# Fused post-LayerNorm block with a top-k mask: a threshold search in three steps instead of five, and a new order of setup and first steps

## The reference, cut to what matters

```python
# x: 8 x 512 x 512, so 4096 tokens of 512; W_syn 2048 x 512; W_out 512 x 2048
x = layernorm(x + x @ (W + delta_W).T)
z = x @ ternary_quant(W_syn).T + b_syn                  # 2048 columns a token
topv, _ = top_k(z, 204); thresh = topv[:, -1:]
hidden = where(z >= thresh, relu(z), 0.0)
out = layernorm(x + hidden @ ternary_quant(W_out).T + b_out) * gamma + beta
return layernorm(x + out)
# ternary_quant(W) = clip(round(W / mean|W|), -1, 1) * mean|W|
```

## Time and profile before

| | us |
|---|---|
| median of 3 runs | 699.13 |
| lowest and highest | 698.31, 703.47 |
| the profiled execution | 703.11 |
| its span (first to last instruction) | 701.3 |
| busy: TensorE, VectorE, ScalarE, GpSimd | 593.7, 538.3, 526.1, 348.9 |
| granted TensorE clock, mean over the span | 0.924 |

### The profile page before, as it was taken

One profiled execution on the slowest core, in us unless ns is written; L12 is line 12 of the kernel. 1 busy time (PEld: TensorE's weight loads), 2 busy tenths in 40 slices (PEclk: granted clock), 3 DMA queues, 4 the chain that ended last, 5 costly groups with the idle time before them and its releaser, 6 DMA issues.

```text
span 701.3 us, 8155 instructions
## 1 busy us (share of the span) xinstructions
PE 593.7 (85%) x2374; PEld 258.3 (37%) x2374; DVE 538.3 (77%) x646; ACT 526.1 (75%) x659; POOL 348.9 (50%) x721
## 2 busy tenths in 40 slices
PE   0777896999999999999999999999999987544443
PEld 0233342444444444444444444444444432211111
DVE  4671866688888888888888888888888888676651
ACT  2335477679989989988998998998998988854322
POOL 0103731246556556555556556556556566555541
PEclk9887897999999999999999999999999999767767
DMA  8931021446454555554546554555444543333331
GB/s 344 390 89 46 15 61 25 95 76 121 91 121 90 122 90 121 91 121 91 120 91 100 112 120 79 121 81 128 91 89 88 88 98 76 75 75 60 76 75 45
DMA packets 184480, 71.61 MB, mean 102 GB/s; under 512 B 168048, under 2 KB 176240, under 8 KB 183792
## 3 DMA queue, kind: packets, MB, share of 16 engines
q1 hardware_dynamic: 184432, 71.07, 45.6%
HBM read 20.72 MB, written 8.39 MB: 42 GB/s over the span
## 4 chain that ended last, share of the span: by engine, by line
PE 28%; POOL 18%; issue 15%; DMA 5%; DVE 4%; ACT 2%; DVEq 1%; POOLq 0%; ACTq 0%
PE o_ps L786 9%; PE z_ps L776 8%; PE o_ps L792 7%; DMA hT<-hh 5%; POOL nmean L328 4%; PE u_ps L762 4%; POOL rs L337 3%; POOL x1b L345 2%; DVE z_sb L691 2%; POOL b L340 2%; ACT hh L500 2%; POOL x1g L349 1%; DVEq L672 1%; POOL dev L364 0%; POOL tmp L369 0%
## 5 line engine op out<-in xcount | busy, mean ns | idle before, releaser
L476 ACT ACTIVATE junk<-z_sb,t_col 128x2048 f16<-128x2048 f32 x128 | 254.8, 1992 | 43.2 <-POOL t_col L383 43.2
L776 PE MATMUL z_ps<-t_syn,xhT 128*128 128x512 f16 x1024 | 226.2, 379 | 0.6 <-issue 0.6
L786 PE MATMUL o_ps<-t_out,hT 128*128 128x512 f16 x512 | 127.7, 407 | 54.4 <-DMA hT<-hh 54.4
L762 PE MATMUL u_ps<-weff,xT_sb 128*128 128x512 f32 x256 | 135.3, 677 | 33.3 <-ACT x1s L483 16.7
L345 POOL TENSOR_TENSOR x1b<-x1s,vecs 128x512 f32<-128x512 f32 x32 | 40.6, 1270 | 234.1 <-DVE z_sb L691 234.1
L776 PEld LDWEIGHTS z_ps<-t_syn,xhT 128*128 128x128 f16 x1024 | 100.0, 98 | 131.8 <-issue 18.5
L657 DVE SCALAR_TENSOR_TENSOR z_sb<-z_ps,sc,bias_z 128x1024 f32<-128x1024 f32 x64 | 81.6, 1278 | 51.6 <-PE z_ps L776 51.6
L792 PE MATMUL o_ps<-t_out,hT 128*128 128x512 f16 x512 | 115.8, 379 | 0.9 <-DMA hT<-hh 0.9
L691 DVE SCALAR_TENSOR_TENSOR z_sb<-z_sb,thr 128x2048 f32<-128x2048 f32 x32 | 75.3, 2352 | 31.1 <-DVE flag L670 18.2
L786 PEld LDWEIGHTS o_ps<-t_out,hT 128*128 128x128 f16 x512 | 52.3, 104 | 124.0 <-DMA hT<-hh 56.6
L500 ACT ACTIVATE hh<-z_sb 128x2048 f16<-128x2048 f32 x32 | 61.1, 1908 | 40.9 <-DVE z_sb L691 39.9
(11 more groups left out here) (114 smaller groups left out, 494.6 us busy)
## 6 DMA issues: line engine op xcount, KB each, us to landing
xT_sb<-in_xT SPq DMA_DIRECT2D x16, 512.0 KB, 4.8
out_y<-y_sb SPq DMA_DIRECT2D x32, 256.0 KB, 2.4
z_sb<-in_w_synT SPq DMA_DIRECT2D x4, 1024.0 KB, 13.3
z_sb<-in_w_outT SPq DMA_DIRECT2D x2, 1024.0 KB, 18.9
hh<-in_w_outT SPq DMA_DIRECT2D x2, 1024.0 KB, 13.7
weff<-in_wT SPq DMA_DIRECT2D x1, 1024.0 KB, 5.4
w_sb<-in_dwT SPq DMA_DIRECT2D x1, 1024.0 KB, 7.6
bias_z<-in_b_syn SPq DMA_DIRECT2D x1, 1024.0 KB, 17.7
```

The lines of the kernel that those rows point to most:

```text
L476: a_.activation(junk[:, done[0] % 2, :], z_sb[:, t % ZS, :], ACT.Sign, bias=bias, scale=-1.0, accum_out=signs[:, t % CS:t % CS + 1]).then_ ...
L762: last = mm(u_ps[:, :], xT_sb[:, j, k, (t % 2) * P:(t % 2 + 1) * P], weff[:, k, :], start=k == 0, stop=k == KD - 1)
L776: last = mm(z_ps[:, c, b * BANK:(b + 1) * BANK], xhT[:, j, h * KD + k, :], t_syn[:, k, n0:n0 + BANK], start=k == 0 and h == 0, stop=k == K ...
L786: mm(o_ps[t % OS][:, :], hT[:, j, 0, c, :], t_out[:, c, :], start=c == 0, stop=False)
```

## The change

Each tile now has its five counts in three steps (`L_SEL` 4 to 2, and all later stages two steps nearer; LAST is 36). In its own step it has count 0, then ScalarE makes the second threshold itself (first_step, a 128 x 1 activation from count 0), then count 1. In the next step it has count 2 and count 3, in the one after count 4. GpSimd makes two batches of updates a step: update_mid for the one tile between its counts 2 and 3, and update_both for the tiles between counts 1 and 2 and between 3 and 4; both are the same 11 operations, on 1 and on 3 columns. `t_col` has two slots, by step parity; `sign_first` and `sign_last` hold the sums of counts 0 and 4. first_step has neither the gate (no move within 8.5 of the aim) nor the floor T_MIN that an update has. reset now comes after count 0 and x1b waits for `below` rather than for hidden. ScalarE's order in a step becomes: counts 2 and 4, the squares, count 3, ln1_out, hi_x, ln3_out, count 0, first_step, count 1, hi_h. GpSimd's: update_mid, scales, x1b, x1g, reset, update_both, means. VectorE's and TensorE's order in a full step stays, and SP's.

In setup ScalarE makes one side of W_syn's ternary form (sign_syn) and VectorE the other, joined by a maximum; the orders of ScalarE, VectorE and TensorE before step 0 are written out; spread comes before the loop; |W_out|'s third and fourth quarter are summed by VectorE; mm2 of tile 0 is split around mm1 of tile 2; scale_vecs moves to step 0.

The diff's core, moved 8 columns to the left. In the ScalarE and VectorE loops only the new state is shown; count_no(t, r) is the place of count r of tile t in ScalarE's order.

```diff
-L_SEL, L_MM3, L_LN2, L_OUT = 4, 5, 6, 7
+L_SEL, L_MM3, L_LN2, L_OUT = 2, 3, 4, 5
-ZS, XS, OS, CS = 6, 9, 3, ROUNDS
+ZS, XS, OS, CS = 6, 7, 3, 3
...
+    def update_mid(s, t):
+        c = slice(t % CS, t % CS + 1)
+        pool.wait_ge(counted, count_no(t, 2))
+        update(t_col[:, s % 2, c], t_col[:, s % 2, c], ng[:, c], signs[:, c], dev[:, 1, c], dev[:, 0, c])\
+            .then_inc(updated_mid, 1)
     def reset(t):
-        c = t % CS
-        step(g.tensor_copy(t_col[:, c:c + 1], start[:, 1:2]))
-        step(g.tensor_copy(ng[:, c:c + 1], start[:, 2:3]))
-        last = step(g.memset(dev[:, t % 2, c:c + 1], 0.0))
-        pool.wait_ge(update_step, last)
+        c = slice(t % CS, t % CS + 1)
+        pool.wait_ge(counted, count_no(t, 0))
+        step(g.tensor_copy(ng[:, c], start[:, 2:3]))
+        g.tensor_scalar(dev[:, 0, c], sign_first[:, t % 2:t % 2 + 1], SIGN_MID, None, ALU.add).then_inc(t_reset, 1)
+        pool.wait_ge(t_reset, t + 1)
+    def update_both(s):
+        if live(s):
+            pool.wait_ge(counted, count_no(s, 1))
+        else:
+            pool.wait_ge(counted, count_no(s - 1, 3))
+        wait(pool, updated_mid, upto(s - 1))
+        wait(pool, selected, upto(s - 3))
+        update(t_col[:, (s + 1) % 2, :], t_col[:, s % 2, :], ng[:, :], signs[:, :], dev[:, 0, :], dev[:, 1, :])\
+            .then_inc(updated, 1)
...
     for s in range(FIRST, LAST + 1):
-        if s == -1:
+        if s <= 2 and live(s + A_LN1):
+            scales(s)
+        if s == -A_LN1:
             bias_norm()
         if s == 0:
             sigma()
-        if 1 <= s <= TILES + ROUNDS - 2:
-            update(s)
-        if live(s):
-            reset(s)
-        if live(s + A_LN1) or live(s - L_LN2) or live(s - L_OUT):
+            scale_vecs()
+        if live(s - 1):
+            update_mid(s, s - 1)
+        if s > 2 and (live(s + A_LN1) or live(s - L_LN2) or live(s - L_OUT)):
             scales(s)
         l, d = s + 1 - L_MM3, s + 1 - L_LN2
-        if s == 2:
-            scale_vecs()
         if live(s - L_SEL):
-            pool.wait_ge(h_made, s - L_SEL + 1)
+            pool.wait_ge(masked, s - L_SEL + 1)
         if live(l):
             if l == 0:
                 pool.wait_ge(vecs_made, 1)
             add_bout(l)
         if live(d):
             add_beta(d)
+        if live(s):
+            reset(s)
+        if live(s) or live(s - 1):
+            update_both(s)
         if live(d) or live(d - 1):
             means(s + 1)
...
+    def sign_syn(i):
+        c, k = divmod(i, KD)
+        act.wait_ge(scaled, 1)
+        wait(act, t_syn_made, i - 3)
+        a_.activation(side[i % 4], syn_in[k][:, c * HALF:(c + 1) * HALF], ACT.Sign, bias=sc[:, 2:3])\
+            .then_inc(over, 1)
...
+        elif r == 1:
+            act.wait_ge(t_first, t + 1)
+            at, signed = t_col[:, s % 2, t % CS:t % CS + 1], signs[:, t % CS:t % CS + 1]
...
+    def first_step(s, t):
+        act.wait_ge(counted, count_no(t, 0))
+        a_.activation(t_col[:, s % 2, t % CS:t % CS + 1], sign_first[:, t % 2:t % 2 + 1], ACT.Identity,
+                      bias=start[:, 3:4], scale=start[:, 2:3]).then_inc(t_first, 1)
...
+    square1(-2, 0)
+    sign_syn(0)
+    sign_syn(1)
+    ln1_out(-2, 0)
+    hi_x(0)
+    sign_syn(2)
+    sign_syn(3)
+    square1(-1, 1)
+    sign_syn(4)
+    ln1_out(-1, 1)
+    hi_x(1)
+    sign_syn(5)
+    sign_syn(6)
+    sum_nnz()
+    sign_syn(7)
+    sum_out(0)
+    square1(0, 2)
+    sum_out(1)
+    ln1_out(0, 2)
+    hi_x(2)
+    for s in range(LAST + 1):
+        f, d, e, a = s - L_SEL, s - L_LN2, s - L_OUT, s + A_LN1
+        if s in (1, 2):
+            square1(s, a)
+        if live(s - 1):
+            count(s, s - 1, 2)
+        if s in (1, 2):
+            ln1_out(s, a)
+            hi_x(a)
         if live(f):
+            count(s, f, 4)
+        if live(a) and s > 2:
+            square1(s, a)
+        if live(d):
+            square2(s, d)
+        if live(e):
+            square3(s, e)
         if live(s - 1):
+            count(s, s - 1, 3)
+        if live(a) and s > 2:
+            ln1_out(s, a)
+            hi_x(a)
+        if live(e):
+            ln3_out(s, e)
+        if live(s):
+            count(s, s, 0)
+            first_step(s, s)
+            count(s, s, 1)
         if live(f):
             hi_h(f)
...
+    def syn_weights(i):
+        c, k = divmod(i, KD)
+        below_lo = neg_syn[:, (i % 2) * HALF:(i % 2 + 1) * HALF]
+        wait(dve, t_syn_made, i - 1)
+        link(v.tensor_scalar(below_lo, syn_in[k][:, c * HALF:(c + 1) * HALF], sc[:, 2:3], -1.0, ALU.is_lt, ALU.mult))
+        dve.wait_ge(over, i + 1)
+        v.tensor_tensor(t_syn[:, k, c * HALF:(c + 1) * HALF], side[i % 4], below_lo, ALU.max).then_inc(t_syn_made, 1)
...
+    def sum_out(k):
+        dve.wait_ge(out_loaded[k], 16)
+        link(v.scalar_tensor_tensor(w_sb[:, :], out_in[k], -1.0, out_in[k], ALU.mult, ALU.max,
+                                    accum_out=pout[:, k:k + 1]))
...
+    for i in range(3):
+        syn_weights(i)
+    lo_x(0)
+    for i in range(3, 6):
+        syn_weights(i)
+    lo_x(1)
+    for i in range(6, 8):
+        syn_weights(i)
     scaling()
+    spread()
+    for s in range(LAST + 1):
+        f, l, d, a = s - L_SEL, s - L_MM3, s - L_LN2, s + A_LN1
         if live(l):
             lo_h(l)
+        if live(s):
+            evac(s, 0)
+        if s == 1:
+            out_scale()
+            out_weights(0)
+        if live(s):
+            evac(s, 1)
         if s == 0:
+            lo_x(a)
+            sum_out(2)
+            sum_out(3)
             out_part()
+        if s == 1:
+            lo_x(a)
+            out_weights(1)
         if live(f):
             below(f)
             top8(f)
             select(f)
+        if live(a) and s > 1:
+            lo_x(a)
+        if s == 2:
+            out_weights(2)
         if live(f):
             general(f)
+        if s == 2:
+            out_weights(3)
+        if live(f):
             hidden(f)
...
+    mm1(0)
+    total(o_ps[0][:, 0:3], part[:, :], part_summed, 1)
+    mm1(1)
+    pe.wait_ge(t_syn_made, KD)
+    mm2(0, 0)
+    total(o_ps[1][:, 0:1], nsyn[:, :], nnz_summed, 1)
+    mm1(2)
+    pe.wait_ge(t_syn_made, 2 * KD)
+    mm2(0, 1)
...
         if live(n):
             mm2(n, 0)
+            if s == 0:
+                total(o_ps[2][:, 0:1], part_out[:, :], part_summed, 2)
             mm2(n, 1)
```

More of the change, by code:

```diff
@@ L109, in postln_kernel @@
         b3 = sb("b3", [P, 2])
-        t_col = sb("t_col", [P, CS])
+        t_col = sb("t_col", [P, 2, CS])
         ng = sb("ng", [P, CS])
@@ L115, in postln_kernel @@
         signs = sb("signs", [P, CS])
+        sign_first = sb("sign_first", [P, 2])
+        sign_last = sb("sign_last", [P, 2])
         tmp = sb("tmp", [P, 8, CS])
@@ L164, in postln_kernel @@
         scaled = sem("scaled")
+        over = sem("over")
         t_syn_made = sem("t_syn_made")
@@ L213, in mean_no, with count_no @@
             return s - L_LN2 + 1
-        def counts_to(s):
-            return sum(upto(s - r) for r in range(ROUNDS))
+        def count_no(t, r):
+            s = t + (0, 0, 1, 1, 2)[r]
+            whole = 2 * upto(s - 1) + 2 * upto(s - 2) + upto(s - 3)
+            new, old, oldest = live(s), live(s - 1), live(s - 2)
+            order = [2] * old + [4] * oldest + [3] * old + [0, 1] * new
+            return whole + order.index(r) + 1
         block = ctx.enter_context(nc.Block())
@@ L356, in step, with update @@
                 return steps_made[0]
[L358 to L364, removed]
+            def update(to, t_old, slope, signed, old, new):
+                q = [tmp[:, k, 0:slope.shape[-1]] for k in range(8)]
+                made_dev = step(g.tensor_scalar(new, signed, SIGN_MID, None, ALU.add))
                 pool.wait_ge(update_step, made_dev)
@@ L714, in _ @@
             first_sums()
-            for c in range(2):
-                for k in range(KD):
-                    ternary(t_syn[:, k, c * HALF:(c + 1) * HALF], syn_in[k][:, c * HALF:(c + 1) * HALF],
-                            sc[:, 1:2], sc[:, 2:3], t_syn_made, c * KD + k)
-                lo_x(c)
+            for i in range(3):
[6 more added lines that the diff above has]
+                syn_weights(i)
             scaling()
-            for s in range(FIRST, LAST + 1):
-                m, f, l, d = s, s - L_SEL, s - L_MM3, s - L_LN2
+            spread()
+            for s in range(LAST + 1):
+                f, l, d, a = s - L_SEL, s - L_MM3, s - L_LN2, s + A_LN1
                 if live(l):
                     lo_h(l)
-                if live(m):
-                    evac(m, 0)
-                    evac(m, 1)
+                if live(s):
[5 more added lines that the diff above has]
+                    evac(s, 1)
                 if s == 0:
-                    spread()
+                    lo_x(a)
+                    sum_out(2)
+                    sum_out(3)
                     out_part()
```

(3 more changed lines are left out.)

136 lines of the change are left out of this document (51 added, 85 removed).

## The result

| | before | after |
|---|---|---|
| median | 698.72 us (697.28 to 703.47) | 737.85 us (737.59 to 738.88) |
| ratio | | 1.0574, 95% interval 1.0533 to 1.0616 |
| span of the profiled execution | 701.3 us | 736.8 us |

The forecast was 721 us in a range of 662 to 742: the sign and the mechanism held, the size was 17 us short. The loss was forecast at 22 us and came to 39, and 737.85 lies 3 us above the 710 to 735 that belonged to the forecast alone. The wide range also took in the opposite outcome, the middle at 17.6 us a step, so that the time lies inside it says little; the rows of one step say more.

What follows compares the result with a forecast made beforehand. TensorE bounds the middle before; after, GpSimd's updates held up by VectorE do. 96.5 + 549.7 + 3 x 19.06 + 20.0 = 723.4 us span, 725.2 with what lies around it, less 4.0 gives 721 us; range 662 to 742.

Steps and rivals of the forecast that it cites:

- setup and fill, to the first mm3_hi: Start of the kernel until mm3_hi(0): 96.5 us (92 to 104 if single terms slip) against 128.1 before.
- 28 full steps: Middle, step 3's start to step 31's: lo_h and `below` hold up GpSimd's updates, 19.75 us a settled step, 549.7 in all.
- three drain steps: Steps after the middle, loop kept as before: 19.06 us each, three instead of five.
- tail: End of the kernel after the drain steps, unchanged by the change: 20.0 us.
- from span to time: From profiled span to median time: add 1.8 us around the span, take off 4.0 for the profiled execution above its median.
- two SBUF inputs: VectorE and GpSimd: a GpSimd operation starting during a VectorE operation with two SBUF inputs stands until that ends.
- Rival 1: Middle: update_both's last steps precede lo_h, or ports do not tie them; 17.6 us a step, 664 us; chance 0.26.
- near tie: Middle, with TensorE leading: update_both's last operation starts at 2.2 us after hidden, lo_h at 2.05.
- Rival 2: Middle: only part of the steps escape lo_h; 18.2 to 19.2 us a step, 681 to 709 us; chance 0.11.
- break-even: Middle: the change neither gains nor loses at 28 steps of 18.9 us.
- Rival 3: Middle: TensorE granted 1.2 GHz in part of each step; 20.3 to 21 us, 738 to 757; 0.08 together with rival 4.
- rival 4: first_step without gate and floor lets candidates miss; VectorE's general path runs, at least 60 us a tile; 2 in 100.

Runs made afterwards that it cites:

- run 1: Kernel after the change, with VectorE's lo_h made to wait until update_both of the step before is through: 697.5 us.
- run 2: Kernel after the change, with lo_h's subtraction replaced by a maximum of equal length reading one SBUF tile, low part of hidden left out: 699.17 us.
- run 4: Kernel after the change, with VectorE's setup sums and ternary work on W_out replaced by one-input maxima of the same length: 723.47 us.
- run 6: run 5's kernel, with W_out's last quarter summed by ScalarE in step 1 and each out_weights waiting until GpSimd's current update is through: 709.61 us.
- run 3: Kernel after the change, with evac(s, 0) put ahead of lo_h on VectorE and no wait added: 716.89 us.
- run 5: run 1's kernel, with GpSimd making x1b between update_mid and the scales: 716.86 us.

## Why the prediction held in kind and missed in size

| term | predicted | measured | |
|---|---|---|---|
| setup and fill, to the first mm3_hi | 96.5 | 109.6 | +13.1 |
| 28 full steps | 549.7 | 547.2 | -2.5 |
| three drain steps | 57.2 | 58.7 | +1.5 |
| tail | 20.0 | 21.3 | +1.3 |
| span | 723.4 | 736.8 | +13.4 |
| from span to time | -2.4 | +1.1 | +3.5 |

The last row is a term of its own: the forecast took off 4.0 us because the profiled execution of the kernel before stood that much above its median; that of the kernel after stands 1.0 above.

**The full step: right.** 19.75 us was the price once the phases had settled, 19.54 the mean and 19.6 the commonest value. update_both is cut at its ninth operation, with eight through; the forecast had seven or eight. `below` cuts update_mid: count 3 waits 0.29 more, forecast 0.46. hidden covers reset. TensorE stands 1.45 and 0.4 us, forecast 1.5 and 0.7. first_step takes 0.39 us, forecast 0.34; the 0.37 estimated from the figures of the Trainium skill ("ScalarE: Activation LUTs", section "What ACT_TABLE_LOAD costs") is the nearer. The first three steps took 19.2, 18.6 and 19.9 us, where the forecast had 17.5, 18.8 and 19.6: the first mm3_hi had itself waited 5.26 us for its transpose, so TensorE did not lead even there. The -2.5 us of the 28 steps are thus +1.7 in the first three and -4.2 in the other 25.

That it is what lo_h reads and not VectorE's time is what runs 1 and 2 show, with evac to rule out what it writes: run 1 takes the meeting away, run 2 the second input, and they give 40 and 39 us. Of run 1's 39.6 us of span, 34.9 lie in the 28 steps (512.3 us against 547.2), 1.1 ahead of them (the scatter of the first count named under run 4), and 3.5 in drain and tail (76.5 against 80.0), where the kernel after has two more cuts of update_both (1.64 us at 668.98, 2.22 at 672.74). The rule of the Trainium skill, "SBUF — State Buffer", section "SBUF: two separate sides", an exclusive lock for the whole instruction, agrees with the cut operations' ends (0.06 to 0.09 us after VectorE's) and with nmean at 0.23 beside the maximum.

**The term that was too small: "hidden(0) ends near 90.1 ... mm3_hi(0) starts at 96.5".** The prediction counted the length of out_weights on VectorE's own path and nothing of what these operations, and the two sums of W_out's quarters, do to GpSimd beside them, though the earlier trace rows was the very place where it had read how near a meeting can be. GpSimd in steps 0 and 1 of the kernel after (reset's second operation, update_both's last two, update_mid's eighth and ninth):

```profile
58.52 2.29 POOL L407 TENSOR_SCALAR dev<-sign_first 128x1 f32<-128x1 f32 x1
...
63.07 1.10 POOL L391 TENSOR_TENSOR tmp<-t_col,tmp 128x3 f32<-128x3 f32 x1
64.26 2.34 POOL L393 TENSOR_SCALAR t_col<-tmp 128x3 f32<-128x3 f32 x1
...
70.69 1.24 POOL L387 TENSOR_TENSOR ng<-ng,tmp 128x1 f32<-128x1 f32 x1
72.01 2.31 POOL L389 TENSOR_TENSOR tmp<-tmp,ng 128x1 f32<-128x1 f32 x1
```

Two of these, the 1.10 and the 1.24 us, stand under the comparison that opens each out_weights:

```profile
62.84 1.29 DVE L705 TENSOR_SCALAR hT<-hh,sc 128x2048 f16<-128x2048 f32 x1
...
70.60 1.28 DVE L705 TENSOR_SCALAR hT<-hh,sc 128x2048 f16<-128x2048 f32 x1
```

It reads one tile (`sc` is one value a row), so the prediction's wording, two SBUF inputs, is too narrow, and the operation of the earlier trace rows was already of this kind. Every operation of this form in these traces that a short GpSimd operation met held it; it runs 2048 columns in 1.29 us where the others need 2.3. No run takes it away alone. And the counts that wait for them:

```profile
53.73 2.00 ACT L525 ACTIVATE junk<-z_sb,start 128x2048 f16<-128x2048 f32 x1 [0.96 <-DVE z_sb L745]
...
66.63 2.00 ACT L525 ACTIVATE junk<-z_sb,t_col 128x2048 f16<-128x2048 f32 x1 [7.68 <-POOL t_col L393]
...
74.93 2.00 ACT L525 ACTIVATE junk<-z_sb,t_col 128x2048 f16<-128x2048 f32 x1 [4.97 <-POOL t_col L393]
```

In these steps no work of other tiles lies between the counts, so each cut is on the path that sets the end. Run 4 puts 9.3 of the 13.1 us down to them; run 6 gets 10.2 back with W_out's work complete. The first count at 53.7, forecast 51 to 52, is another 2 us, and the rest, under 2 us, is not assigned. The late count begins with mm2 of tile 0, which starts at 38.77, after 6.37 us of idle for its transpose. That transpose was issued at 30.07 and took 8.6 us to land, the next two 3.1 and 3.4; before, it was issued at 33.25 and took 5.2. So the earlier handoff won nothing there. From 30 to 39 us the DMA engines are fully busy in both traces (a share of 1.09 as the profile counts it), with weights among others; that the transpose waited for them fits, but no run tests it.

**The rivals.** Rival 1 put the middle at 17.6 if update_both's last operations got in ahead of lo_h. In the settled step its last operation would have begun at 359.72 (357.37, where update_both starts, and the 2.35 us from first to last of run 1) against lo_h's 359.06, 0.66 us too late; the forecast had 0.5 or more for that state, and the near tie it feared needed TensorE in the lead, which it did not have. But where update_both is not cut, in runs 1 and 2, the middle does not come to 17.6 either, since `var` and `ok` are next: the forecast had no term for them, and rival 1's 664 us did not follow from its own condition. What it said of the state, that one loss leads to the one in which lo_h leads, is what the 26 cuts in a row from step 5 on show. Rival 2 did not come about: from the third step on none took less than 19.4 us. With the setup as measured, run 1's mean of 18.30 us a step makes no more than a tie with the kernel before, where the forecast had the break-even at 18.9. Rival 3, whose times began at 738 us, would fit the time alone, but not the clock of 0.99 in the middle; it did not come about, nor did rival 4 (VectorE's general path has no instruction in the trace).

## To carry to other kernels

A chain of small GpSimd operations costs its length plus, for each operation that starts while VectorE reads two SBUF tiles (or runs a comparison of the earlier trace rows's kind), what is left of VectorE's operation; so lay out the start of each chain against VectorE's long operations in every stage, the setup too, and let VectorE wait, 0.3 us in run 1, rather than cut the chain. After each such edit look where the next meeting falls: an order that mends one can bring about another (runs 3 and 5), and what counts is which operation stands in the queue when VectorE's begins, one that is wanted at once (`var`) or one that is wanted later (b). Fewer steps at the ends pay only if the full step keeps its price: here 2 us more in each of 28 steps outweighed them.

## What was not expected of the hardware

The meeting costs VectorE as well. A GpSimd operation over 512 columns, x1g, made VectorE's one-column `ok` 1.13 us instead of 0.22 (run 1), and `below` 3.44 instead of 2.34 when x1b and it began 0.02 us apart (run 5). The trace of the kernel before had this in the earlier trace rows, unread: lo_h begins under x1g and takes 2.68 us there, and 2.29 in every step of the kernel after. That x1b began 0.02 us behind `below` by the records and still went first; 0.09 us behind was too late: L387 at 355.91 behind `below` at 355.82, in run 3, took 2.31 us.
